# First expert stage of a two-layer gated cross-attention and mixture-of-experts kernel: gate and up products as three fp32r products of split operands

## The reference

```python
def _moe_forward(x, moe_router, moe_w13, moe_w2):      # 8 experts, TOP_K = 2, MOE_DIM = 512
    ...
    w13_out = jax.lax.ragged_dot(x_sort, moe_w13, group_sizes)      # (6400, 256) x (8, 256, 1024)
    gate, up = jnp.split(w13_out, [MOE_DIM], axis=-1)
    hidden = jax.nn.silu(gate) * up
    out_dispatch = jax.lax.ragged_dot(hidden, moe_w2, group_sizes)  # (6400, 512) x (8, 512, 256)
    out_flat = jnp.zeros_like(x_flat).at[token_ids_sort].add(out_dispatch * w_sort[:, None], mode='drop')
x = x + jnp.tanh(g_ffn[0]) * _moe_forward(_layernorm(x), ...)
```

## Time and profile before

| | |
|---|---|
| median of 3 executions | 2190.73 us (2183.68 to 2193.98) |
| the profiled execution | 2188.08 us, its span 2186.4 us |
| busy: PE, DVE, POOL, ACT | 1981.3, 1301.8, 1260.8, 912.1 us |
| first expert stage, DVE's first step of the plan | 736.44 us |
| its first transposes on TensorE | 749.33 us |
| its last down products start | 1086.27 us |

### The profile page before, as it was taken

The page is one execution under the profiler, slowest core; times in us unless marked ns, Lnnn a source line. Parts: engine busy times, 40 slices in busy tenths (PEclk is TensorE's granted clock), DMA queues, the critical chain, the costliest instruction groups (busy, mean ns, idle before and its releaser), DMA issues. The chain is left out here.

```text
span 2186.4 us, 39576 instructions
## 1 busy us (share of the span) xinstructions
PE 1981.3 (91%) x11190; PEld 1295.9 (59%) x11190; DVE 1301.8 (60%) x3986; ACT 912.1 (42%) x2313; POOL 1260.8 (58%) x1488
## 2 busy tenths in 40 slices
PE   3999999999999499999859999999999559999897
PEld 2777777777776266666525555555555325555554
DVE  3677777777776222221147888888887435555554
ACT  1444344444443122222227666666666213333332
POOL 1344444444444244444437888888888537777776
PEclk9999999999999699999969999999999569999999
DMA  4110101101134022232301111111116255455444
GB/s 129 35 37 27 39 26 38 39 26 39 28 105 175 19 44 44 46 48 44 47 27 35 36 36 32 36 35 36 36 35 200 67 149 79 75 78 79 75 79 73
DMA packets 143796, 127.45 MB, mean 58 GB/s; under 512 B 48505, under 2 KB 134241, under 8 KB 143590
## 3 DMA queue, kind: packets, MB, share of 16 engines
q0 software_dynamic: 39456, 46.11, 13.2%
q1 hardware_dynamic: 96348, 70.67, 11.5%
q10 hardware_dynamic: 7786, 8.14, 1.2%
HBM read 87.16 MB, written 37.65 MB: 57 GB/s over the span
## 5 line engine op out<-in xcount | busy, mean ns | idle before, releaser
L747 POOL TENSOR_SCALAR prob<-prob,rc 100x363 f32<-100x363 f32 x256 | 158.7, 630 | 342.9 <-DVE rc L610 342.9
L1617 PE MATMUL psG<-expert_w,xgT 128*128 x688 | 329.7, 602 | 2.5 <-ACT xgT L1558 2.2
L1643 PE MATMUL psD<-expert_w,hT 128*128 x916 | 230.9, 385 | 2.8 <-ACT hT L1575 2.8
L1430 POOL DMA_INDIRECT xg<-xn,slots x178 | 175.5, 986 | 100.3 <-issue 49.7
L1443 POOL DMA_INDIRECT out<-y,slots x115 | 185.2, 1611 | 71.9 <-DVE y L1524 26.1
L1558 ACT ACTIVATE xgT<-psX 128x256 f32<-128x256 f32 x172 | 66.1, 384 | 361.8 <-PE psX L1605 361.8
L1443 POOL DMA_INDIRECT acc<-y,slots x57 | 89.7, 1574 | 173.0 <-DVE y L1524 169.2
L937 PE MATMUL psJ<-wkv,cTn 96*121 96x512 f32 x384 | 177.6, 600 | 0.0
L1643 PEld LDWEIGHTS psD<-expert_w,hT 128*128 128x128 f32 x916 | 160.4, 190 | 21.6 <-issue 4.7
L1617 PEld LDWEIGHTS psG<-expert_w,xgT 128*128 128x128 f32 x688 | 118.8, 193 | 88.4 <-issue 88.4
L536 ACT ACTIVATE prob<-psS,nm 100x361 f32<-100x361 f32 x256 | 141.8, 561 | 54.1 <-DVE nm L605 50.9
(11 more groups left out here) (256 smaller groups left out, 4708.8 us busy)
## 6 DMA issues: line engine op xcount, KB each, us to landing
expert_w<-in_L_ffn_moe_w SPq DMA_DIRECT2D x8, 1024.0 KB, 13.8
xn<-xm SPq DMA_DIRECT2D x64, 100.0 KB
bias<-in_L_ffn_b ACTq DMA_DIRECT2D x3, 2048.0 KB, 13.9
ctx<-in_ctx SPq DMA_DIRECT2D x32, 181.5 KB
cT<-in_ctxT SPq DMA_DIRECT2D x32, 180.5 KB
cT<-in_ctxT SPq DMA_DIRECT2D x64, 90.2 KB
expert_w<-in_L_ffn_moe_w SPq DMA_DIRECT2D x8, 512.0 KB, 12.9
expert_w<-in_L_ffn_W1T SPq DMA_DIRECT2D x16, 256.0 KB
```

Of the source, the lines that this page charges most:

```text
L747: g.tensor_scalar(prob[:, q, :], prob[:, q, :], rc[:, q:q + 1], 1.0, ALU.mult, ALU.mult).then_inc(prob_done, 1)
L1430: g.indirect_dma_start(xg[:, j % 4, :], None, xn_rows, bass.IndirectOffsetOnAxis(slots[:, j % RING, 0:1].bitcast(U32), 0)).then_inc(gather ...
L1617: mm = t.matmul(psG[:, r, :], xT[:, r, k, :], w13[:, bass.ds(e, 1), k, 0:512], start=k == 0, stop=k == 1)
L1643: mm = t.matmul(psD[:, r, 0:D], hT[:, r, k, :], w2[:, bass.ds(e, 1), k, :], start=k == 0, stop=k == KF - 1)
```

## The change

In the first expert stage each weight of `w13` and each gathered, transposed row is split into a part rounded to fp32r and the rest of it. A product x w becomes x_hi w_hi + x_lo w_hi + x_hi w_lo, three fp32r products that accumulate in the same PSUM bank. The rounded weights need a new tile of 64 KB in each partition (`w_hi`); the rest is written over the weights in place. At the start of the stage ACT makes `w_hi` for one expert after another, GpSimd subtracts for experts 0 and 1 ahead of its first gather, DVE for experts 2 to 7 behind the plan, and TensorE waits for all eight ahead of its first transposes. In the loop ACT's copy of the transposed rows makes `x_hi`, and DVE has a new step `low` for `x_lo`, ahead of `weighted` and `hidden`; TensorE's products and the next transposes wait for it (`x_low`) where they waited for ACT (`x_out`). The down products and the second expert stage stay as they are.

```diff
@@ experts
-        xT = sb("xgT" + L, [P, 2, 2, P])
+        if L0:
+            w_hi = sb("w13_hi", [P, E, 2, 2 * F], F32R)
+            x_hi, x_lo = sb("xg_hi", [P, 2, 2, P], F32R), sb("xg_lo", [P, 2, 2, P], F32R)
+        else:
+            xT = sb("xgT" + L, [P, 2, 2, P])
@@ GpSimd, ahead of g.wait_ge(plan_done, 1) and the first gather
+                if L0:
+                    for e in range(2):
+                        g.wait_ge(w_high, e + 1)
+                        g.tensor_tensor(w13[:, e].bitcast(F32R), w13[:, e], w_hi[:, e].bitcast(F32), ALU.subtract).then_inc(w_low, 1)
@@ VectorE, behind the plan
-                if not L0:
+                if L0:
+                    for e in range(2, E):
+                        v.wait_ge(w_high, e + 1)
+                        v.tensor_tensor(w13[:, e].bitcast(F32R), w13[:, e], w_hi[:, e].bitcast(F32), ALU.subtract).then_inc(w_low, 1)
+                else:
                     v.wait_ge(bias_in, 16 * 3)
+
+                def low(j):
+                    v.wait_ge(x_out, j + 1)
+                    v.tensor_tensor(x_lo[:, j % 2, :, :], psX[:, 0:2 * P].rearrange("p (k n) -> p k n", k=2),
+                                    x_hi[:, j % 2, :, :].bitcast(F32), ALU.subtract).then_inc(x_low, 1)
...
+                if L0:
+                    low(0)
                 hidden(0)
                 for j in range(NT):
+                    if L0 and j + 1 < NT:
+                        low(j + 1)
                     if j >= 2:
                         weighted(j - 2)
@@ ScalarE
-                    s.activation(xT[:, j % 2, :, :], psX[:, 0:2 * P].rearrange("p (k n) -> p k n", k=2), ACT.Copy).then_inc(x_out, 1)
+                    s.activation(x_hi[:, j % 2, :, :] if L0 else xT[:, j % 2, :, :], psX[:, 0:2 * P].rearrange("p (k n) -> p k n", k=2), ACT.Copy).then_inc(x_out, 1)
...
-                if not L0:
+                if L0:
+                    s.wait_ge(w_loaded, w_total)
+                    for e in range(E):
+                        s.activation(w_hi[:, e], w13[:, e], ACT.Copy).then_inc(w_high, 1)
+                else:
@@ TensorE
                     if j >= 1:
-                        t.wait_ge(x_out, j)
+                        t.wait_ge(x_low if L0 else x_out, j)
...
+                def split(ps, r, e, cols):
+                    for k in range(2):
+                        hi, lo = w_hi[:, bass.ds(e, 1), k, cols], w13[:, bass.ds(e, 1), k, cols].bitcast(F32R)
+                        t.matmul(ps, x_hi[:, r, k, :], hi, start=k == 0, stop=False)
+                        t.matmul(ps, x_lo[:, r, k, :], hi, start=False, stop=False)
+                        mm = t.matmul(ps, x_hi[:, r, k, :], lo, start=False, stop=k == 1)
+                    return mm
...
+                    t.wait_ge(x_low, j + 1)
                     if j >= 2:
-                    ...
+                        t.wait_ge(g_out, j - 1)
+                    split(psG[:, r, :], r, e, slice(0, F)).then_inc(g_mm, 1)
+                    if j >= 2:
+                        t.wait_ge(hid_done, j - 1)
+                    split(psU[:, r, :], r, e, slice(F, 2 * F)).then_inc(u_mm, 1)
...
                 t.wait_ge(w_loaded, w_total)
+                if L0:
+                    t.wait_ge(w_low, E)
                 x_transpose(0)
```

More of the change, by code:

```diff
@@ L1414, in experts @@
         slots_in = [sem(f"slots_in{q}_{L}") for q in range(4)]
-        gathered, bias_in = [sem(f"gathered{q}_{L}") for q in range(4)], sem("bias_in" + L)
+        gathered, bias_in = [sem(f"gathered{q}_{L}") for q in range(4)], None if L0 else sem("bias_in1")
         scattered = [sem(f"scattered{q}_{L}") for q in range(2)]
@@ L1419, in experts @@
         x_out, g_out, h_out = sem("x_out" + L), sem("g_out" + L), sem("h_out" + L)
-        pre_done, hid_done, yb_done, y_done = sem("pre_done" + L), sem("hid_done" + L), sem("yb_done" + L), sem("y_done" + L)
+        if L0:
+            x_low, w_high, w_low = sem("x_low"), sem("w13_high"), sem("w13_low")
+        hid_done, y_done = sem("hid_done" + L), sem("y_done" + L)
+        if not L0:
+            pre_done, yb_done = sem("pre_done1"), sem("yb_done1")
         with nc.Block() as block:
@@ L1606, in x_transpose @@
                     mm.then_inc(x_mm, 1)
+                def split(ps, r, e, cols):
[5 more added lines that the diff above has]
+                    return mm
                 def up(j, e):
                     r = j % 2
-                    t.wait_ge(x_out, j + 1)
-                    if j >= 2:
[L1612 to L1624, removed]
+                    if not L0:
+                        t.wait_ge(x_out, j + 1)
+                        if j >= 2:
+                            t.wait_ge(pre_done, j - 1)
+                        for k in range(2):
+                            mm = t.matmul(psG[:, r, :], xT[:, r, k, :], w13[:, bass.ds(e, 1), k, 0:512], start=k == 0, stop=k == 1)
+                        mm.then_inc(g_mm, 1)
+                        return
+                    t.wait_ge(x_low, j + 1)
+                    if j >= 2:
+                        t.wait_ge(g_out, j - 1)
+                    split(psG[:, r, :], r, e, slice(0, F)).then_inc(g_mm, 1)
+                    if j >= 2:
+                        t.wait_ge(hid_done, j - 1)
+                    split(psU[:, r, :], r, e, slice(F, 2 * F)).then_inc(u_mm, 1)
                 def h_transpose(j):
```

## The result

The kernel after takes 2166.54 us (median of four executions, 2163.14 to 2168.25), the kernel before on the same chip 2190.2 us (median of four, 2183.68 to 2193.98). The ratio is 0.9896, its 95% interval 0.988 to 0.9912: about 1% faster, near the 2171 us that were forecast. The profiled execution took 2168.25 us, its span 2166.5, 19.9 us less than the span before.

A forecast was written before the change was run, and what follows sets the result against it. TensorE's matmul array was taken as the bound, tile after tile. Products -34.2, first tiles +1.4 and start +14.2 gave -18.6 us: 2188.08 to 2169.5, as a median 2172.1, written 2171 us; range 2159 to 2182.

The forecast's parts named there:

- 12 x 0.23 + 0.08 = 2.84 us instead of 3.44: Gate and up products of a tile: twelve fp32r for four fp32, 0.60 us less, 34.2 us over 57 tiles.
- the 0.08 for the change from fp32 to fp32r: TensorE, once a tile: the first fp32r product after an fp32 instruction takes 0.31 us, 0.08 more than 0.23.
- the forecast's 0.47 more: First three tiles, without down products as cover: the wait for the rows' rest costs 3 x 0.47 = 1.4 us.
- 34.2 - 1.4 = 32.8: Whole stage behind its start: 34.2 us saved by the products, less 1.4 us for the first three tiles.
- The start: Start of the stage: splitting the weights makes the first transposes 14.2 us later, 11.0 or 18.0 at GpSimd's price ends.
- the ratio to DVE of the small shape, 1.7: GpSimd's subtraction of 2048 columns, priced from a 256-column row against DVE: 3.9 us, ends 2.29 and 5.8.
- The form of the stall: Plan of tiles: two-input DVE steps wait for GpSimd's subtractions, so the plan ends at 749.6, not 742.2.
- B (no lock): Rival, start of the stage: plan steps are not held by GpSimd, start 6.7 us late, 2163 us; chance 0.22.
- C (0.31 us for each product): Rival, gate and up products: each takes 0.31 us, weight load not fetched ahead; 2221 us, chance 0.06.
- D (the loop's floor): Rival: gather and scatter loop keeps the period at 5.82 us, 2204 us, chance 0.03; milder form 2176 to 2185, 0.11.
- The sum for the profiled execution: Whole kernel: -34.2 + 1.4 + 14.2 = -18.6 us on the profiled 2188.08 us, which makes 2169.5.

The follow-up runs named there:

- experiment 3: The changed kernel with all eight weight subtractions on DVE behind the plan, none on GpSimd: 2165.6 us, ratio 0.99.
- experiment 4: The changed kernel with GpSimd's two subtractions moved behind the plan, ahead of its first gather, DVE keeping six: 2166.01 us, ratio 0.9906.
- experiment 6: The changed kernel with two of each three fp32r products (8 a tile), 2113.31 us, then with one of three (4 a tile), 2074.05 us; results differ.
- experiment 1: The changed kernel without the split of the weights, the loaded weights standing in for both parts (result differs): 2151.93 us, ratio to before 0.9838.
- the kernel with two tiles early: The changed kernel with all eight subtractions on DVE and the first two tiles each waiting only for their own expert's split: 2156.0 us, ratio 0.985.
- the kernel with one tile early: The changed kernel with all eight subtractions on DVE and the first tile let in when its own expert is split: 2160.2 us, ratio 0.9853.

## Why the prediction was right

**The tiles.** The step was "12 x 0.23 + 0.08 = 2.84 us instead of 3.44", a period of 5.22 us. The period was 5.17. The products cost what the earlier trace rows show: eleven of them take 909.40 - 906.86 = 2.54 us, 0.231 each. (The forecast says that each product of the earlier trace rows has another stationary tile; two pairs of the five there share one. Here each of the twelve differs from the one ahead of it, and the price is the same.) The term that was mis-sized is the 0.08 for the change from fp32 to fp32r. From the hidden transposes to the second product the trace after has 0.68 us, where transposes and one product are 0.43 + 0.23 = 0.66: the change costs 0.02. The first fp32r product is 0.33 us ahead of the second because it begins 0.08 us sooner behind the transposes (0.35 for 0.43), and this distance was read as a price. Over some 54 tiles this is 3 us.

**The first tiles.** The waits for the rest of the rows were there, three of them, 1.02, 1.02 and 0.58 us; the rows came at 1.68 us for 1.22 in the first tile, the forecast's 0.47 more. What the sum left out: in the first tile the clock is still low (the granted clock of 766 to 772 us is 0.59, before it was 0.58 from 750 to 757), and there the products take 4.67 us (767.01 to 771.68) for 6.16, a gain of 1.5 and not 0.6. Timeline of the first tile's products before, up to the next transposes:

```profile
750.55 3.77 PE L1617 MATMUL psG<-expert_w,xgT 128*128 x4 [0.56 <-ACT xgT L1558]
...
756.71 0.38 PE L1605 MATMUL psX<-ident,xg 128*128 128x128 f32 x2
```

Together with the 3 us this explains that the stretch behind the first transposes fell by 36.6 us and not by 34.2 - 1.4 = 32.8.

**The start.** 14.74 us, forecast 14.2. Its parts were off and partly made up for one another. GpSimd's subtraction takes 4.5 us, forecast 3.9: the ratio to DVE of the small shape, 1.7, is 2.0 in the large one. DVE's six come 2.22 us apart (2.29 is the length of one record, and the records overlap), ACT's copies 1.81 (1.95; the forecast's own slope gives 1.97). The form of the stall was right to the step: the eleventh and the thirteenth of the plan wait, each for nearly a whole instruction of GpSimd. That GpSimd is the cause is shown by experiment 3, which takes its subtractions away (no stretch, though ACT's copies still run), and by experiment 4, which moves them (the stretch moves along).
"GPSIMD Engine Reference" in the Trainium skill, Elementwise — side-by-side cycle accounting, has 4.50 us for an add of two fp32 tiles of 2048 columns; the trace has 4.50 for the subtraction (9.00 for two), so its figure was nearer than the estimate from the nearest row.

**The rivals.** B (no lock) is excluded by experiments 3 and 4. C (0.31 us for each product) is excluded by the trace; the queue of TensorE keeps up with twelve products at computed addresses. D (the loop's floor) is excluded at 5.82 us by the period of 5.17, and down to 3.5 us by experiment 6.

The sum for the profiled execution was -18.6 us, and -19.9 was measured. The stage itself came out 3.3 us better than the sum (3 from the tiles, 0.9 from the first tile's products, less 0.5 at the start), and 2.0 of it went in stretches that the change does not touch. That the whole comes within 1.3 us of the sum is partly luck.

## What to carry to other kernels

Where fp32 products of 512 columns bound the time, three fp32r products in place of each cost about four fifths of it (a tile lost 0.65 of 3.44 us), and making the rest of the gathered rows is free as long as DVE does it while TensorE has other work. The preparation is what costs: count it as time at the start of the stage, look at which instructions it stands beside, and start the consumers on the parts that are ready. A helper engine that can't run beside the first one can cost more than it takes over: here GpSimd's two eighths made the start longer by 3.9 us.

## What was not expected of the hardware

GpSimd's instruction for an indirect gather takes 0.94 to 1.00 us by itself (experiment 1), but 1.74 to 1.89 beside DVE's subtractions with both inputs in SBUF. By line, those from 750 to 775 us of the kernel after (ns min/median/max), and then the first six of experiment 1:

```profile
L1438 POOL DMA_INDIRECT xg<-xn,slots x6: 940/1796/1892, 755.4 to 772.8; - x6
```

```profile
L1438 POOL DMA_INDIRECT xg<-xn,slots x6: 942/947/1003, 746.9 to 758.2; - x6
```

In experiment 3, where GpSimd has no subtraction of its own, six such take 945 to 1892 ns, 1808 in the middle: it is DVE's subtractions that hold the instruction up. In the kernel after this costs nothing, as TensorE waits for the subtractions anyway; in the kernel with two tiles early the second tile's transposes wait 1.51 us for their gather.

The clock can be lost again within the start of the stage. Windows of the kernel with one tile early (us, busy time of PE, PEld, DVE, ACT, POOL, granted clock, DMA share, GB/s):

```profile
754.00:756.00 2.00, 2.00 (x6) 1.54 (x6) 2.00 (x2) 0.60 (x1) 1.70 (x2) 0.50 0.13 31
756.00:758.00 2.00, 1.13 (x5) 0.55 (x3) 2.00 (x2) 0.00 (x0) 1.24 (x1) 0.93 0.15 47
...
760.00:762.00 2.00, 0.35 (x2) 0.29 (x2) 0.82 (x1) 0.00 (x0) 0.00 (x0) 0.50 0.00 0
...
764.00:766.00 2.00, 2.00 (x6) 1.57 (x5) 0.00 (x0) 0.00 (x0) 0.01 (x1) 0.50 0.25 74
```

The clock rose from 1.2 GHz (0.50) to 2.4 GHz during the first tile's products (0.93 in the window of the rise), TensorE then had nothing to do for some 4.5 us, and the second tile began at 1.2 GHz again: its first seven products start 0.43 us apart and not 0.23, and the twelve take 4.33 us where those of the second tile of the kernel after take 2.85. With two tiles early the third tile's products start 0.43 us apart at first too, after three microseconds with few instructions (762.76 to 765.76). Whether the early tiles' gain would be larger with TensorE kept busy in between was not tried.
